# State-space stage: the logarithm series in PSUM, another order in the tail, constant-tile products there, and the low-rank weights loaded during that stage

## The reference

```
x = x + tanh(g_xattn[0]) * ssm(ctx, layernorm(x), ...)
x = x + tanh(g_ffn[0])   * lora_moe(layernorm(x), A, B, Wr, br)
...
ssm:  x = in_proj_w @ ctx;  u = silu(causal_conv4(x) + conv_b)
      dt_lo, B, C = split(x_proj_w @ u)
      delta = softplus(dt_proj_w @ dt_lo + dt_proj_b);  A = -exp(A_log)
      state = state * exp(delta * A) + (delta * u) * B;  y = state . C      (per token, 16 states)
      y = (y + D * u) * silu(z)
lora: logits = x @ Wr.T + br; the expert with the highest probability, weighted by it
      y = (x @ A[e].T) @ B[e].T / 64
```

## Time and profile before

| | us |
|---|---|
| median of 3 runs | 1026.83 |
| lowest, highest | 1024.70, 1027.12 |
| the profiled execution's own time | 1026.77 |
| its span (first to last instruction) | 1025.0 |
| PE busy | 889.4 (87%) |
| DVE busy | 707.8 (69%) |
| ACT busy | 609.5 (59%) |
| POOL busy | 403.5 (39%) |
| mean granted clock of PE, share of full | 0.948 |

### The profile page before, as it was taken

The page is one execution under the profiler, slowest core; times in us unless marked ns, Lnnn a source line. Parts: engine busy times, 40 slices in busy tenths (PEclk is TensorE's granted clock), DMA queues, the critical chain, the costliest instruction groups (busy, mean ns, idle before and its releaser), DMA issues. The chain is left out here.

```text
span 1025.0 us, 17396 instructions
## 1 busy us (share of the span) xinstructions
PE 889.4 (87%) x5612; PEld 554.8 (54%) x5612; DVE 707.8 (69%) x1405; ACT 609.5 (59%) x1196; POOL 403.5 (39%) x339
## 2 busy tenths in 40 slices
PE   9599948999999999997697688998649999957697
PEld 4455535624777777775376553332425666644445
DVE  6989957889766676666788658995452334248875
ACT  5589944687777777776564366888303433205472
POOL 2798610376545454542231280000023676310132
PEclk9899979999999999999899799999869999979989
DMA  2332029000000000000000201400393333240001
GB/s 84 106 124 99 6 107 345 12 1 16 17 20 15 21 17 21 15 15 4 3 1 1 58 2 54 134 2 2 118 354 88 64 72 47 32 118 0 1 1 42
DMA packets 44239, 57.29 MB, mean 56 GB/s; under 512 B 5656, under 2 KB 35104, under 8 KB 44176
## 3 DMA queue, kind: packets, MB, share of 16 engines
q1 hardware_dynamic: 37680, 48.33, 14.0%
q0 software_dynamic: 4416, 6.03, 3.5%
q10 hardware_dynamic: 2080, 2.10, 0.6%
HBM read 49.90 MB, written 6.49 MB: 55 GB/s over the span
## 5 line engine op out<-in xcount | busy, mean ns | idle before, releaser
L1413 POOL TENSOR_TENSOR a_scratch<-a_scratch,a_inverse 128x512 f32<-128x512 f32 x64 | 66.5, 1039 | 115.2 <-DVE a_inverse L1549 115.2
L2626 PE MATMUL bank<-wup,moe_xT 128*128 x184 | 83.0, 594 | 1.3 <-ACT moe_xT L2688 1.2
L2410 DVE TENSOR_REDUCE a_tops<-bank 128x4 f32<-128x1024 f32 x64 | 77.7, 1223 | 8.5 <-PE bank L2090 5.5
L2861 DVE TENSOR_TENSOR moe_act_f<-bank,moe_silu 128x512 f32<-128x512 f32 x23 | 15.9, 692 | 92.4 <-ACT moe_silu L2695 80.6
L2258 ACT ACTIVATE wup<-bank,a_exp_scale 128x1024 f32<-128x1024 f32 x64 | 71.2, 1114 | 13.7 <-PE bank L2113 13.7
L567 POOL TENSOR_TENSOR ssm_drive<-ssm_du,ssm_b_row 128x1024 f32<-128x1024 f32 x32 | 75.6, 2392 | 8.4 <-DVE ssm_state L638 4.6
L638 DVE TENSOR_TENSOR_SCAN ssm_state<-bank,ssm_drive 128x512 f32<-128x512 f32 x64 | 74.8, 1209 | 1.1 <-issue 0.4
L1332 ACT ACTIVATE a_scratch<-bank,a_bias,a_q_factor 128x256 f32<-128x256 f32 x128 | 71.1, 560 | 7.1 <-DVE a_bias L1536 6.8
L1144 PE MATMUL bank<-keys,a_scratch 128*128 (+1 forms) x256 | 68.6, 390 | 2.0 <-DVE xn L1476 0.7
L2688 ACT COPY moe_xT<-bank 128x256 f32<-128x256 f32 x23 | 8.6, 373 | 99.5 <-PE bank L2614 99.5
L412 PE MATMUL bank<-ssm_seen,ident 128*128 128x512 f32 x124 | 65.8, 614 | 1.1 <-ACT ssm_seen L502 1.1
(11 more groups left out here) (504 smaller groups left out, 2336.0 us busy)
## 6 DMA issues: line engine op xcount, KB each, us to landing
ssm_b_row<-ssm_b_spill SPq DMA_DIRECT2D x16, 512.0 KB, 3.6
wup<-in_l_up_dram SPq DMA_DIRECT2D x8, 1024.0 KB, 10.0
a_wq_in<-in_l1x_q_dram SPq DMA_DIRECT2D x32, 128.0 KB, 2.1
wdn<-in_l_down_dram SPq DMA_DIRECT2D x8, 512.0 KB, 11.1
keys<-in_l1x_o_dram SPq DMA_DIRECT2D x1, 2048.0 KB, 12.1
X<-in_x_dram SPq DMA_DIRECT2D x1, 1024.0 KB
lora_raw<-in_l_gate_dram SPq DMA_DIRECT2D x1, 1024.0 KB, 7.0
lora_raw<-in_l_up_dram SPq DMA_DIRECT2D x1, 1024.0 KB, 9.0
```

The costliest lines, as they stand in the source:

```text
L1413: pool.tensor_tensor(prob[:, j, :, :], prob[:, j, :, :], inverse[:, j, :].unsqueeze(2).to_broadcast([P, 2, SEQ]), ALU.mult).then_inc(S["p_ ...
L2410: dve.tensor_reduce(tops[:, f // 2 % 3, :, first:first + 2].rearrange("p q h -> p h q"), bank[:, at:at + 2, :].rearrange("p h (q n) -> p h ...
L2626: last = pe.matmul(bank[:, 2 * (i % 2) + m, :], xT[:, i % 2, c, :], wup[:, bass.ds(e, 1), c * 2 * FF + m * FF:c * 2 * FF + (m + 1) * FF] . ...
```

## The change

- The series is evaluated in PSUM banks 4 and 5 in place of `conv` in SBUF. For this DVE first waits until `chained` and `w_c_ready` have passed (bank 5 is free) and, for k = 1, until the copy of k = 0 is done.
- PE's `skip_term(0)` and `skip_term(1)`, which write banks 4 and 5, move behind the transposes of z and wait for both `delta_ready`. `keep_busy(8)` becomes `keep_busy(4)`.
- In the tail PE makes all four transposes of the last state before `gather(14, 3)`. ACT loads its table and makes gates and two silus before it weighs (15, 2). After all four `y_ready` PE multiplies 12 times on the tile of zeros into bank 2.
- The low-rank weights get tensors that live from the start until the BitNet stage ends. SP loads them early in the state-space stage, after POOL has cleared `low_R`; the low-rank stage waits on `low_in` in place of `loaded`.

```diff
+    def hold_low_rank(self, ctx):
+        self.low_A, self.low_B, self.low_R = sb("low_A", [P, DC, HALF]), sb("low_B", [P, HALF // P, DM]), sb("low_R", [P, DC, 32])
+        self.low_bias, self.low_rank8 = sb("low_bias", [P, 8]), sb("low_rank8", [P, 8])
+        self.low_in = self.nc.alloc_semaphore(name="low_in")
...
-        series, sums = conv, conv
+        sums = conv
...
                 sp.dma_start(core.identh[:, :], d["identh"]).then_inc(S["gates_s"], 16)
+                sp.wait_ge(S["low_clear"], 1)
+                sp.dma_start(core.low_R[:, :, 0:8], d["l0_Wr"].rearrange("(c p) e -> p c e", p=P)).then_inc(core.low_in, 16)
+                sp.dma_start(core.low_bias[:, :], d["l0_br"].partition_broadcast(P)).then_inc(core.low_in, 16)
+                sp.dma_start(core.low_rank8[:, :], d["rank8"]).then_inc(core.low_in, 16)
+                sp.dma_start(core.low_A[:, :, :], d["l0_A"].rearrange("(c p) e -> p c e", p=P)).then_inc(core.low_in, 16)
+                sp.dma_start(core.low_B[:, :, :], d["l0_B"].rearrange("(c p) e -> p c e", p=P)).then_inc(core.low_in, 16)
                 sp.wait_ge(S["blank_set"], 1)
...
-                skip_term(0)
-                skip_term(1)
                 pe.wait_ge(S["rows_ready"], 1)
...
+                pe.wait_ge(S["delta_ready"], CC)
+                skip_term(0)
+                skip_term(1)
                 await_emptied(pe, ("z", 2))
-                keep_busy(8, ring((0, 0)))
-                for q, previous in zip(rounds[ROUNDS:-2], [None] + rounds[ROUNDS:-3]):
+                keep_busy(4, ring((0, 0)))
+                for q, previous in zip(rounds[ROUNDS:-4], [None] + rounds[ROUNDS:-5]):
                     turn(q)
-                    if previous is not None and previous not in direct:
+                    if previous is not None:
                         gather(*previous)
-                turn((LAST, 2))
-                turn((LAST, 3))
+                for r in range(ROUNDS):
+                    turn((LAST, r))
+                gather(LAST - 1, 3)
                 gather(LAST, 2)
                 gather(LAST, 3)
+                pe.wait_ge(S["y_ready"], ROUNDS)
+                keep_busy(12, 2)
...
-                weigh(LAST, 2)
                 act.preload_act_table_set("silu_and_others")
...
                 for r in range(ROUNDS):
+                    if r == 2:
+                        weigh(LAST, 2)
                     act.wait_ge(S["act_emptied"], emptied["z", r])
...
                 pool.memset(core.blank[:, :], 0.0).then_inc(S["blank_set"], 1)
+                pool.memset(core.low_R[:, :, :], 0.0).then_inc(S["low_clear"], 1)
...
                     dve.wait_ge(S["e_ready"], k + 1)
-                    chain(dve.tensor_scalar(series[:, k, :], small[:, k, :], LOG1P[0], None, ALU.mult))
+                    dve.wait_ge(S["chained"], 1)
+                    await_count(dve, S["delta_ready"], k)
+                    dve.wait_ge(S["w_c_ready"], 1)
+                    series, e = bank[:, 4:6, :], two(small[:, k, :])
+                    chain(dve.tensor_scalar(series, e, LOG1P[0], None, ALU.mult))
                     for c in LOG1P[1:]:
-                        chain(dve.scalar_tensor_tensor(series[:, k, :], series[:, k, :], c, small[:, k, :], ALU.add, ALU.mult))
+                        chain(dve.scalar_tensor_tensor(series, series, c, e, ALU.add, ALU.mult))
...
-                    dve.copy_predicated(delta[:, k, :], is_small[:, k, :].bitcast(mybir.dt.uint32), series[:, k, :]
+                    dve.copy_predicated(two(delta[:, k, :]), two(is_small[:, k, :]).bitcast(mybir.dt.uint32), series
...
low-rank stage:
-                sp.wait_ge(padded, 1)
-                (the five loads, as above)
-                pe.wait_ge(loaded, 5 * 16)
+                pe.wait_ge(core.low_in, 5 * 16)
-                pool.memset(wR[:, :, :], 0.0).then_inc(padded, 1)
```

More of the change, by code:

```diff
@@ L66, in __init__ @@
         self.blank = sb("blank", [P, DM])
+    def hold_low_rank(self, ctx):
+        sb = lambda name, shape, dt=F32: ctx.enter_context(self.nc.sbuf_tensor(name, shape, dt))
+        self.low_A, self.low_B, self.low_R = sb("low_A", [P, DC, HALF]), sb("low_B", [P, HALF // P, DM]), sb("low_R", [P, DC, 32])
+        self.low_bias, self.low_rank8 = sb("low_bias", [P, 8]), sb("low_rank8", [P, 8])
+        self.low_in = self.nc.alloc_semaphore(name="low_in")
     def hold_ternary(self, ctx):
@@ L276, in stage_ssm @@
         b_spill = nc.dram_tensor("ssm_b_spill", [NS, NTOK], F32).ap()
-        names = ("in_s", "w_s", "ident_s", "x_s", "gates_s", "set_up", "blank_set",
+        names = ("in_s", "w_s", "low_clear", "ident_s", "x_s", "gates_s", "set_up", "blank_set",
                  "in_done", "tapped", "conv_done", "u_ready", "x_turned", "w_xT_ready", "chained", "w_c_ready",
@@ L718, in stage_lora_moe @@
     with core.stage("lora") as s:
-        wA, wB, wR = s.sb("wA", [P, DC, ER]), s.sb("wB", [P, JC, DM]), s.sb("wR", [P, DC, 32])
-        bias, rank8 = s.sb("bias", [P, NE]), s.sb("rank8", [P, NE])
+        wA, wB, wR, bias, rank8 = core.low_A, core.low_B, core.low_R, core.low_bias, core.low_rank8
         lg, e8, rank, hot = (s.sb(n, [P, NT, NE]) for n in ("lg", "e8", "rank", "hot"))
@@ L733, in stage_lora_moe @@
         sums, sums_out = s.sem("sums"), s.sem("sums_out")
-        loaded, padded, l_summed, l_brought, logits, shifted, exps, chained = (s.sem(n) for n in (
-            "loaded", "padded", "l_summed", "l_brought", "logits", "shifted", "exps", "chained"))
+        l_summed, l_brought, logits, shifted, exps, chained = (s.sem(n) for n in (
+            "l_summed", "l_brought", "logits", "shifted", "exps", "chained"))
         core.vo_in = s.sem("vo_in")
@@ L891, in _ @@
                 mid = lambda a: a.unsqueeze(1).to_broadcast([P, NT, NE])
-                dve.wait_ge(loaded, 5 * 16)
+                dve.wait_ge(core.low_in, 5 * 16)
                 dve.wait_ge(logits, 1)
@@ L3327, in build @@
         core = Core(nc, ctx, dram)
[L3328 to L3335, removed]
+        with ExitStack() as low:
+            core.hold_low_rank(low)
+            stage_ssm(core)
+            with ExitStack() as held:
+                core.hold_ternary(held)
+                with ExitStack() as keys:
+                    core.hold_keys(keys)
+                    stage_lora_moe(core)
+                    stage_attention_16(core)
+                stage_bitnet(core)
         with ExitStack() as held:
```

## The result

| | before | changed |
|---|---|---|
| median of 7 runs, us | 1026.78 | 1015.26 |
| lowest, highest | 1024.01, 1028.83 | 1011.00, 1018.95 |
| span of the profiled execution | 1025.0 | 1016.9 |

The ratio over all runs is 0.9897, interval 0.9875 to 0.9918: about 10.6 us faster (8.4 to 12.8); the two medians lie 11.5 us apart. The time lies in the stated range. The profiled execution of the changed kernel took 1018.60, 3.3 us above its median, that of the kernel before 1026.77, its median; what follows is read from these two.

The account below looks back on a forecast made before the run. The touched stages were taken as a chain: DVE's series sets the first scan, PE and DVE bound the steps. Gains of 6.5 + 2.3 + 1.95 + 4.4 = 15.1 us took 1026.77 to 1011.7, range 1008.8 to 1016.5.

Parts of the forecast that it names:

- Series: Start of the state-space stage: series in PSUM escapes POOL's contention, first scan at 37.2 for 43.66; gain 6.5 us.
- Skip terms: First step: moved skip terms and four products keep PE warm into the state transposes, fourth weighing at 46.8; 2.3 us more.
- The rival's price for a cold PE: First state transpose: PE is cold, the 2.33 us wait stays, total 1014.0; chance 14%.
- Steps: From 55.35 to 129.39 PE and DVE are both the bound; the change leaves this work alone, no gain counted.
- Tail: End of the state-space stage: reordered transposes, gathers and ACT work end DVE's close 3 at 135.5 for 137.47; gain 1.95 us.
- Low-rank stage: Warm PE and early loads remove the load wait and half-clock products before DVE's coefficients; gain 4.4 us.
- They keep pace: Low-rank stage: the raw weights' loads start 2.4 us earlier with 1 MB less ahead, so they keep pace.
- The sum: Whole kernel: 6.5 + 2.3 + 1.95 + 4.4 = 15.1 us off 1026.77, giving 1011.7.
- a microsecond taken from it moves the rest: The stages up to 190 us are a chain, and nothing behind them waits for an absolute time.
- an interval from there to the end of the kernel that is not the old one: Sign of being wrong: the span from the low-rank stage's first DVE addition to the kernel's end differs from before.
- the rivals: PE cold 14%, low-rank gain lost 12%, series partly contended 5%, slower 3%; also the end not moving.

Follow-up runs that it names:

- experiment 11: The kernel before plus four products on the tile of zeros at PE's end in the low-rank stage: 1026.45 us over 12 runs, ratio 0.9997.
- experiment 1: The changed kernel with the series back in the SBUF tile conv, all else as changed: 1018.3 us (before 1024.55).
- experiment 2: The changed kernel with the old order in the tail (PE's last transposes and gathers, ACT's weighing), the 12 products kept: 1018.69 us (before 1024.55).
- experiment 7: The changed kernel with the load of the turned context moved behind the query weights: 1010.84 us (changed beside it 1013.12).
- experiment 8: The changed kernel with both four products at PE's low-rank end and the turned context's load behind the query weights: 1010.99 us, ratio 0.9852.
- experiment 3: The changed kernel without the 12 products after y_ready: 1013.88 us (before 1024.55), ratio 0.9899.
- experiment 6: The changed kernel plus four products on the tile of zeros at PE's end in the low-rank stage: 1010.79 us (changed beside it 1013.12), ratio 0.9860.
- run 5: The changed kernel again, nothing altered: 1013.12 us over 6 runs (before 1025.18).
- run 10: The changed kernel plus four products at PE's end in the low-rank stage, once more: 1011.26 us (changed 1015.18, before 1025.39).
- experiment 4: The changed kernel with the five low-rank loads back at the head of the low-rank stage: 1019.47 us (before 1024.55).
- experiment 9: The changed kernel a third time, nothing altered: 1015.18 us (before 1025.39).

## Why the prediction was right, and where it was not

Measured against its own two profiles, part by part:

- *Series*: 3.77 for 9.85 us as reckoned from L596; first scan forecast 37.2, measured 36.96. Undone, 6.8 us. Right in mechanism and size. The Trainium skill ("VectorE: DVE Perf Modes", "Why PSUM operands drop a tier") says that any PSUM operand costs an fp32 operation its double rate. The trace agrees: the tensor_scalar went from 0.69 to 1.23.
- *Skip terms*: PE free at 41.2 (forecast), first state transpose at 41.05; fourth weighing 46.8, measured 46.48, thus 9.1 us earlier, forecast 8.8. Right, though PE's clock had risen only just before. The size, 2.4 us here, would be 1.3 against the profile of experiment 11. The rival's price for a cold PE was too high, as experiment 1 shows: returning skip terms and products warm it.
- *Steps*: 0 forecast, 0.6 us gained (DVE's weighing before the last state 9.75 earlier). This term was put at nothing. About 0.35 us of it is a halt of DVE ("issue") before 122.62 in the kernel before, which the two other profiles with the series in SBUF have too and the ten with the series in PSUM don't:
```profile
122.62 1.22 DVE L638 TENSOR_TENSOR_SCAN ssm_state<-bank,ssm_drive 128x512 f32<-128x512 f32 x1 [0.39 <-issue]
```
- *Tail*: last product 137.47 to 125.88, so 1.8 us, forecast 1.95. Right; 1.6 by experiment 2.
- *Low-rank stage*: logits 15.81 earlier, so 4.2 us in the stage up to there, forecast 4.4. The whole stage gained 3.5. "They keep pace" failed for the query weights, for which ACT now waits 2.62 us; that this is where the 0.7 us went fits experiment 7 but not experiment 8, and is not shown.
- *The sum*: 15.1 forecast, 15.09 found at the end of the changed code. Each part is near its forecast, but this exact agreement is luck. The 0.9 us too few in the low-rank stage are made up by 0.6 in the steps and 0.3 in the first step, and another execution of the same code before starts its low-rank stage 1.8 us earlier (experiment 11).
- **The step that failed** is the first paragraph's, that "a microsecond taken from it moves the rest". The rest is not of fixed length. In the profiles of the kernels here it was 832.5 us (experiments 1, 3 and 6), 833.5 (8), 834.5 (runs 5 and 10, the kernel before 834.6), 834.8 (7), 836.3 (11), 839.6 (4), 840.2 (9), 841.5 and 841.9 (2), with PE busy from 726.6 to 737.0. I read one execution (834.57) and took it as constant. The prediction named "an interval from there to the end of the kernel that is not the old one" as a sign of being wrong, and that sign came. The range covered it only just, and by luck: it was drawn for the rivals, of which none came true in its profile.

What is shown is that the time given back has two parts.
- *DVE's halt and the steps behind it.* The attention with 16 heads took 294.5 us in the three profiles with the series in SBUF (the kernel before, experiments 1 and 11). It took 296.3 to 296.6 in seven with the series in PSUM, and 298.0 or 298.1 in the three of these kernels whose first products ran at half clock (294.5 + 1.8 + 1.7). The 1.8 us belong to the change. They come and go with DVE's program at the series, and not with PE's four products (experiments 6, 8, 10 and 11) or with the chip (experiments 1 to 4 ran on one). Why DVE halts there is open; no run moved its instructions while leaving the series alone.
- *PE's clock.* Behind the attention the same stages took 538.2, 543.5 and 543.6 us in the three profiles of the changed kernel, and 540.0 and 541.8 in two with the code before. In the 19 executions of the changed kernel the time goes with the mean granted clock, from 1008.79 us at 0.962 to 1018.95 at 0.949. It needs no other placement of tensors and no fall at the attention's first products.

What stays open: why the clock falls more in some executions than in others, and whether the change makes the long ones more frequent (the rest worked out from the medians of all runs is 838 for the changed kernel and 833 for the one before; 1.8 of this difference comes with DVE's program). Open is also why four products at one border help it by 2.3 and 3.9 us in the two groups of runs and the kernel before not visibly. They remove at most 1.7 us at that border. With 9 against 19 runs the difference is unlikely to be luck, but experiment 7 came out as low without any of them, so that other small shifts in time may do the same; their way through the later stages was not traced.

The kernels with the lowest medians: with four products 1010.8 and 1011.3, with the moved load 1010.8, with both edits 1011.0. All are clearly below the kernel before; their intervals overlap with the changed kernel's.

## What to carry to other kernels

Where DVE and POOL work side by side on operations of two SBUF tensors each, look for one whose running operand can live in PSUM: here it took a factor of 2.6 off DVE and a third off POOL. Place work that must be done anyway (skip terms) or empty products directly ahead of PE's return, and make sure that they start before PE has cooled; started late they are themselves on the path (7.13 us for 5.45 in experiment 2). The 12 products brought 2.5 us at their place and nothing that the total shows. Before adding up a gain, compare several executions of the unchanged remainder: its spread (9 us here) is the error of the sum. An edit to one engine's program can also move its halts in stages that it doesn't touch (1.8 us here); compare the lengths of the unchanged stages one by one.

## What the runs showed of the hardware that was not expected

- One kernel's remainder, instruction for instruction the same, took 834.47 and 840.19 us in two executions, with a mean granted clock of 0.96 and 0.94 and the same busy time on DVE within 1.1 us.
- The same 2.0 us of idleness before the attention ended in a clock of 0.5 in three profiles (5.38 us for 16 records) and not in the six others that kept it (3.69 us).
- A scalar_tensor_tensor of 1024 fp32 elements takes 1.23 us with its running operand in PSUM, also beside POOL's two-tensor product, and 1.23 in SBUF without that neighbour, but 3.25 us in SBUF beside it.
- DVE stood idle for 0.36 us with nothing to wait for and then took 1.05 us for an operation on 2 elements, at the same place in ten profiles. In three others, whose DVE program differs more than 200 us earlier, this operation takes 0.41 us, and idle times of 0.34 to 0.39 us of that kind lie elsewhere.
